# x1's product in expert 0's gate product, behind a product of zeros, instead of between the last two down products

## What is computed

```
xn  = LN(x)
s   = attention_1(xn) @ Wo.T                  # 16 heads of 8; weights 1 - tanh(energy)^2, causal
x1  = xn + softmax_attention(rmsnorm(xn)) @ wo
h2  = rmsnorm(x1)
moe = swiglu(h2, shared) + sum over 8 experts of combine[t, e] * swiglu(h2, expert e)    # top 2 of 8
out = x + s * silu(x1 + moe)
```

## Time and profile before

| | |
|---|---|
| median of three runs | 1098.51 us (1096.68 to 1098.54) |
| profiled execution, its own time | 1097.14 us |
| its span | 1095.4 us |
| PE busy | 990.9 us (90%) |
| DVE busy | 831.4 us (76%) |
| ACT busy | 646.8 us (59%) |
| POOL busy | 351.2 us (32%) |
| granted PE clock, mean | 0.982 of full speed |

### The profile page before, as it was taken

One profiled execution on the slowest core, in us unless ns is written; L12 is line 12 of the kernel. 1 busy time (PEld: TensorE's weight loads), 2 busy tenths in 40 slices (PEclk: granted clock), 3 DMA queues, 4 the chain that ended last, 5 costly groups with the idle time before them and its releaser, 6 DMA issues.

```text
span 1095.4 us, 18252 instructions
## 1 busy us (share of the span) xinstructions
PE 990.9 (90%) x6763; PEld 467.3 (43%) x6784; DVE 831.4 (76%) x1684; ACT 646.8 (59%) x882; POOL 351.2 (32%) x211
## 2 busy tenths in 40 slices
PE   4489999899998999889998999989999899988997
PEld 1123464245542455324652346523554245532464
DVE  6885977869776888759878598795977779773962
ACT  3569724786258842698336972379624785258731
POOL 4702443033520355105530154203352033610032
PEclk9589999999999999999999999999999999999999
DMA  7350561023700435105331055211471033600020
GB/s 231 71 109 22 111 169 34 21 55 80 190 20 12 99 93 132 30 2 130 112 83 30 2 130 143 51 31 30 101 181 24 21 79 83 163 20 2 1 79 10
DMA packets 60392, 81.83 MB, mean 75 GB/s; under 512 B 8560, under 2 KB 47728, under 8 KB 57296
## 3 DMA queue, kind: packets, MB, share of 16 engines
q1 hardware_dynamic: 56544, 75.61, 28.3%
q10 hardware_dynamic: 3760, 5.05, 1.4%
HBM read 52.98 MB, written 27.39 MB: 73 GB/s over the span
## 4 chain that ended last, share of the span: by engine, by line
PE 53%; DVE 25%; ACT 12%; issue 4%; DMA 2%; SPq 1%; ACTq 0%; POOL 0%; DVEq 0%; POOLq 0%
PE O L1156 11%; DVE nmax L758 10%; DVE PT L813 9%; PE O L1139 7%; ACT PT L613 7%; PE S L1172 6%; PE S L1174 5%; PE S L1173 5%; PE S L1112 4%; PE M L1075 3%; PE M L1054 2%; PE M L1080 1%; PE O L1075 1%; SPq L368 1%; DMA stackQ<-mTZ 1%
## 5 line engine op out<-in xcount | busy, mean ns | idle before, releaser
L613 ACT ACTIVATE PT<-S 128x1024 f32<-128x1024 f32 (+1 forms) x448 | 417.0, 967 | 113.7 <-PE S L1112 108.7
L813 DVE SCALAR_TENSOR_TENSOR PT<-PT 128x768 f32<-128x768 f32 (+1 forms) x192 | 213.4, 1163 | 101.0 <-ACT PT L613 101.0
L758 DVE TENSOR_REDUCE nmax<-M 128x1 f32<-128x512 f32 x329 | 218.2, 684 | 43.2 <-PE M L1075 28.3
L1139 PE MATMUL O<-PT,V 128*32 128x256 f32 (+3 forms) x2816 | 246.5, 430 | 0.0
L494 POOL TENSOR_TENSOR PT<-PT,CB 128x1024 f32<-128x1024 f32 x56 | 133.6, 2392 | 261.2 <-DVE PT L951 146.9
L646 ACT ACTIVATE PT<-S 128x1024 f32<-128x1024 f32 x72 | 73.9, 1027 | 241.4 <-PE S L1174 241.4
L479 POOL TENSOR_TENSOR split<-split,parts 128x512 f32<-128x512 f32 x30 | 90.9, 3029 | 372.0 <-ACT parts L573 372.0
L1112 PE MATMUL S<-stackQ,stackK 64*128 64x512 bf16 (+3 forms) x1024 | 166.3, 347 | 9.5 <-DMA stackQ<-mTZ 5.3
L758 DVE TENSOR_REDUCE nmax<-O 128x1 f32<-128x512 f32 x183 | 125.1, 684 | 36.5 <-PE O L1075 17.6
L1172 PE MATMUL S<-h2hi,wgu_hi 128*128 128x512 f32 x288 | 148.7, 516 | 4.3 <-DVE PT L951 4.2
L1156 PE MATMUL O<-PT,wdn 128*128 128x512 f32 x288 | 142.9, 595 | 0.9
(11 more groups left out here) (198 smaller groups left out, 1044.5 us busy)
## 6 DMA issues: line engine op xcount, KB each, us to landing
CB<-scrC SPq DMA_DIRECT2D x64, 256.0 KB, 5.6
stackQ<-scrQ SPq DMA_DIRECT2D x30, 384.0 KB, 5.5
stackK<-scrK SPq DMA_DIRECT2D x30, 384.0 KB, 6.3
scrQ<-parts SPq DMA_DIRECT2D x32, 192.0 KB, 3.3
scrK<-parts SPq DMA_DIRECT2D x30, 192.0 KB, 5.9
scrQ<-parts SPq DMA_DIRECT2D x32, 128.0 KB, 3.4
scrK<-parts SPq DMA_DIRECT2D x30, 128.0 KB, 5.2
KX<-scrK SPq DMA_DIRECT2D x14, 192.0 KB, 3.4
```

The lines of the kernel that those rows point to most:

```text
L613: a.activation(PT[:, n % SLOTS, 2 * q * w:2 * q * w + 2 * w].rearrange("p (r n) -> p r n", r=2), S[k][:, :].rearrange("p (r n) -> p r n", ...
L758: v.tensor_reduce(nmax[:, h % 2, h // 2, t:t + 1], M[k][:, :], AX.X, ALU.max, negate=True).then_inc(m_read[k], 1)
L813: v.scalar_tensor_tensor(p, p, 1.0, p, ALU.subtract, ALU.mult).then_inc(weighed, 1)
L1139: last = t_.matmul(O[k][32 * q:32 * q + VW, i0:i1], V[:, j, 4 * g + q, :], PT[:, n % SLOTS, w * q + at:w * q + at + i1 - i0], start=(j == ...
```

## The change

x1's product leaves its place ahead of the last down product. A new function, `x_turned`, runs on PE behind the first step of expert 0's gate product and ahead of `with_v`. It waits for proj2's reader (the writer of x1), for ACT's reading of O[0] and for the clearing of the tile KX, then makes one matmul that opens the accumulation: the lower 64 rows of the bf16 identity against 64 partitions of KX that hold zeros, 512 columns, bf16. The four x1 matmuls follow, without a count of `down_done`. Down 0 no longer opens the accumulation and no longer waits for O[0]. `DOWNS` falls from 10 to 9, and ACT's waits at the row's first units are renumbered to the same down products as before.

```
-DOWNS = NE + 1
+DOWNS = NE
...
-                done = {0: 0, 1: 1, 2: DEPTH}
-                if q == 0 and n in done and it * DOWNS + done[n] > 0:
+                done = {0: 1, 1: 2, 2: DEPTH}
+                if q == 0 and n in done:
                     act.wait_ge(down_done, it * DOWNS + done[n])
...
+            def x_turned(u, it):
+
+                pe.wait_ge(*read(u, "proj2"))
+                pe.wait_ge(o_read[0], it * O_USES[0] + 3)
+                pe.wait_ge(kset, 4)
+                t_.matmul(O[0][:, :], identb[HALF:128, :], KX[HALF:128, 0, 0, :], start=True, stop=False)
+                for t in range(NT):
+                    t_.matmul(O[0][:, t * 128:t * 128 + 128], x1[:, t, :], ident[:, :], start=False, stop=False)
+
             def second_product(it, e):
 
                 if e == 0:
-                    pe.wait_ge(o_read[0], it * O_USES[0] + 3)
                     k, c = score_use(it, 2 * EXPERT + 1)
                     pe.wait_ge(s_read[k], c + 2)
...
                     last = t_.matmul(O[0][:, :], wdn[:, e, f, :], AB[e % DEPTH][:, f * 512:f * 512 + 512],
-                                     start=(e == 0 and f == 0), stop=(e == NE - 1 and f == NFH - 1))
+                                     start=False, stop=(e == NE - 1 and f == NFH - 1))
...
                     for i, _step in enumerate(expert(it, e)):
+                        if e == 0 and i == 0:
+                            x_turned(u, it)
                         if e == 0 and i < 2:
                             with_v(it, UNITS - 2 + i)
...
-                for t in range(NT):
-                    last = t_.matmul(O[0][:, t * 128:t * 128 + 128], x1[:, t, :], ident[:, :], start=False, stop=False)
-                last.then_inc(down_done, 1)
                 for _step in second_product(it, NE - 1):
                     pass
```

## The result

The changed kernel takes 1102.88 us (median of 7 runs, 1100.49 to 1103.48) against 1097.76 us (median of 7, 1096.6 to 1100.76) for the kernel before. The ratio is 1.0042, with a 95% interval of 1.0033 to 1.0052: slower by 4.6 us (3.6 to 5.7). Forecast were +3.85 and 1102.2 us. The forecast time stands on the median of the first three runs of the kernel before, 1098.51 us, so the difference is the fairer comparison: the ratio gives +4.6 us, the two medians +5.1. The profiled execution took 1100.49 us with a span of 1098.8.

What follows compares the result with a forecast made beforehand. PE bounds the experts, DVE waiting for down 8 the row's end. Cost 1.41 less gain 0.91 is +0.50 us for seven rows, plus 0.35 in the last: +3.85, forecast 1102.2 us, range 1098.3 to 1104.6.

Steps and rivals of the forecast that it cites:

- The bound at each place: PE never pauses through experts 0 to 8; at the row's end DVE waits for down 8, idling 1.54 us.
- The gain, 0.91 us: At the row's end: x1's 1.09 us goes, down 8 grows from 1.73 to 1.91; all 0.91 a row arrives.
- The cost, 1.41 us: At expert 0, each row: 0.32 us for the zeros plus 1.09 for x1's product behind them, none swallowed.
- the free and the exposed switches: Tiling changes around the zeros at expert 0: 1.11 us a row if free, 1.41 as forecast, 1.61 with one more exposed.
- the lower bound: Cost at expert 0 with free tiling switches: 0.22 + 0.89 = 1.11 us a row, total 1100.0 us.
- Rival (a): At expert 0 the switches to 64 rows and back hide under the zeros: +1.45 us, 1100.0 or less; chance 0.19.
- Rival (b): PE's 0.50 us wait before expert 2's up product swallows what it can: 0.00 to -0.30 a row; chance 0.12.
- its sign of being wrong (the wait shrinks): PE's 0.50 us wait before expert 2's up product shrinking or vanishing would mean the wait swallows part of the cost.
- (d): A new wait holds, for example for O[0]'s reader: 1 us a row gives +11.9, 1110; chance 0.04 shared with another rival.
- The last row: At the last row 0.17 us is swallowed at cT: +1.24 at expert 0, -0.89 at the end, net +0.35 us.
- The step to cT: In the last row, cT and the CB DMAs hanging on it move by 1.24 us, as 0.17 is swallowed.

Runs made afterwards that it cites:

- the run with both products: The changed kernel with x1's product made at its old place too, so x1 is added twice: 1108.34 us against 1097.95 for the kernel before, ratio 1.0094.
- the runs in expert 2 and unit 26: Changed kernel, x1's product moved to expert 2 behind combT (no zeros: 0.9958) or unit 26 before h2's transposes (no zeros 0.9941, with zeros 0.9929); ratios to kernel before.

## Why the prediction was right

- **The bound at each place** held: with PE's order lengthened in expert 0 every later piece of the row moved, and DVE waited for down 8 at the row's end.
- **The gain, 0.91 us.** Measured by itself it is 0.88. That down 8 inherits the price of the changed tiling was right: 1.93 us in the changed kernel, forecast 1.91. Taking the whole 1.09 would have been the error to make here.
- **The cost, 1.41 us.** The chain shows 0.32 + 1.09, and the run with both products 1.45 a row. (The prediction's sum without any price of a switch, 1.11 - 1.09 = 0.02, leaves the switch in x1's old 1.09; without it there as well, that is 1.11 - 0.89 = 0.22 us a row.) The choice between the free and the exposed switches, the point where the bounds were furthest apart, was right; zeros of full height gave the lower bound (1.12 against 1.11).
- **Rival (a)**, that the switches hide under the zeros, is shown wrong by the run with both products (1.45 us a row, not 1.11). **Rival (b)**, the swallowed wait: at this place the wait stayed. The prediction read it as 0.50 us, which counts a product without a record as idle time; the forecast doesn't suffer, as none of the wait was to be used, but its sign of being wrong (the wait shrinks) would have misled a reader of PE's row alone. In its general form, that a wait of PE can pay for the product, it was right, and the runs in expert 2 and unit 26 show where. **(d)** had no sign in the trace.
- **The last row** was mis-sized: +0.53 us against +0.35. The step to cT is right: from the scaling before it 1050.72 - 973.25 = 77.47 us in the kernel before and 1054.73 - 976.06 = 78.67 after, +1.20 against the 1.24 worked out. But the first CB DMA behind it took 3.37 us and not 3.13, 0.24 more. It takes 3.13 to 3.44 us over the profiled executions of the nine kernels, one each, so whether the change has a part in the 0.24 isn't shown:

```profile
1054.73 0.69 DVE cT L879
...
1057.05 3.37 DMA CB<-scrC
```

- **The total.** In the trace row 0 is 0.51 us longer (from the DMA `stackQ<-mTZ`, at 83.98 and 83.36 us in the two chains, to the scaling at 187.75 and 187.64), the six rows behind it 2.92 together, and the last 0.53. That is +4.0 us, against +3.85 forecast and a timed difference of +4.6 (3.6 to 5.7); all three lie within the interval. The two prices measured apart, 1.45 and 0.88, would give 0.57 a row where the changed kernel's rows show 0.49 on average. These few hundredths are not resolved.

## What to carry to other kernels

A product that is moved within an engine's order costs the part of it that doesn't fit into a wait, and a wait only pays if what it waits for is not itself queued behind the moved work: look one step past the releaser (here cT behind combT) before counting a wait as cover. Before comparing the length of a wait in two traces, see that both have the records just ahead of it. Price small matmuls with their neighbours: a 64-row product put among full-height ones cost more through its two changes of tiling (0.29 us) than through its own columns (0.22), and taking a product away can hand its switch on to the next. Before opening an accumulation with a product of zeros, let the first real product open it, or put the zeros where the engine idles.

## What the runs showed of the hardware

The price of the change back to full height looks like one weight load that isn't done ahead. Behind zeros of full height x1's first load starts 0.23 us ahead of its first matmul:

```profile
391.25 1.09 PEld L1158 LDWEIGHTS O<-ident,x 128*128 128x128 f32 x8
391.48 1.05 PE L1158 MATMUL O<-ident,x 128*128 128x128 f32 x8
```

Behind the 64-row zeros of the changed kernel load and matmul start together:

```profile
392.24 0.97 PEld L1154 LDWEIGHTS O<-ident,x 128*128 128x128 f32 x8 [0.23 <-issue]
392.24 1.16 PE L1154 MATMUL O<-ident,x 128*128 128x128 f32 x8
```

One such load takes 0.19 us, and the switch back to full height costs 0.18 to 0.20. For the 0.10 us to 64 rows the same isn't shown, though a bf16 load takes 0.10: in the kernel before a full-height bf16 product behind an fp32 one has load and matmul together as well, and starts 0.24 us behind the fp32 one (403.31), without any such price:

```profile
403.54 0.10 PEld L1075 LDWEIGHTS M<-KX,stackQ 128*128 128x128 bf16 x1 [0.28 <-issue]
403.55 0.39 PE L1075 MATMUL M<-KX,stackQ 128*128 128x512 bf16 x1
```

No run tried whether the change of tiling itself holds the load back, or something that comes with it.

Single executions of one kernel differ by about as much as the effect (1096.6 to 1100.76 us for the kernel before), and one profiled execution shows how that can come about. In the run without x1's product one row took 132.57 us where its neighbours take 129.9 to 130.2. PE waited 2.03 us for the last row of maxima, a DMA of 2.96 us:

```profile
608.37 0.39 PE L1112 MATMUL S<-stackQ,stackK 64*128 64x512 bf16 x2 [2.03 <-DMA stackQ<-mTZ]
```

and after that idle stretch the granted clock fell to 0.50, that is 1.2 GHz, and it was back at 1.00 (2.4 GHz) by 614 us (each line: stretch, its length, busy time of PE, PEld, DVE, ACT and POOL, then PE's clock, DMA share, GB/s):

```profile
606.00:608.00 2.00, 0.33 (x8) 0.00 (x0) 0.90 (x4) 1.64 (x2) 0.00 (x0) 1.00 0.01 1
608.00:610.00 2.00, 1.63 (x16) 0.55 (x20) 0.00 (x0) 1.10 (x2) 0.00 (x0) 0.79 0.00 0
610.00:612.00 2.00, 2.00 (x18) 0.31 (x12) 0.00 (x0) 1.42 (x2) 0.00 (x0) 0.50 0.00 0
612.00:614.00 2.00, 2.00 (x23) 0.52 (x20) 0.00 (x0) 1.66 (x3) 0.00 (x0) 0.85 0.00 0
```

The same DMA takes 1.67 or 1.68 us in most rows of the kernel before. The five other full rows of that execution show nothing of this. This is why rows were compared above beside the timed runs.
